# Attention and mixture-of-experts layer: the causal mask is added by VectorE in its maximum, and logits and the shared down product take fewer matmuls

## What is computed

```
q = x @ wq                                  # 8 heads of 128, 2 groups of keys and values
k = (x @ wk_down) @ wk_up;  v likewise      # through 32 latent features
scores = q @ k.T * scale                    # 1024 x 1024 for each head
scores = where(causal, scores, min)         # the mask
y = softmax(scores) @ v;  y @ wo

logits = x @ gate_weight.T                  # 32 experts
tw, topidx = top 6 of sigmoid(logits) + bias in the 2 best of 4 groups
routed = sum over experts of cw * (silu(x @ w_gate) * (x @ w_up)) @ w_down
shared = (silu(x @ shared_w_gate) * (x @ shared_w_up)) @ shared_w_down
anchor = the same with 16 smaller experts, the one that topidx names
```

## Time and profile before

| | us |
|---|---|
| median of three runs | 396.92 |
| the profiled execution | 394.98 |
| its span | 393.2 |
| TensorE busy | 374.4 |
| GpSimd busy | 284.0 |
| VectorE busy | 277.7 |
| ScalarE busy | 237.8 |

### The profile page before, as it was taken

How to read it: one execution, slowest core, us unless ns; L and a number is a source line. 1 busy time by engine, 2 the same in 40 slices (tenths; PEclk the granted TensorE clock), 3 DMA queues, 4 the chain that set the end, 5 groups by cost and what they waited for, 6 DMA issues and landing times.

```text
span 393.2 us, 6898 instructions
## 1 busy us (share of the span) xinstructions
PE 374.4 (95%) x2088; PEld 257.5 (65%) x2088; DVE 277.7 (71%) x707; ACT 237.8 (60%) x475; POOL 284.0 (72%) x336
## 2 busy tenths in 40 slices
PE   7989899999999998999999999999999999999992
PEld 7665455555555554455468887788878888788861
DVE  5979599986876983547348866759766677567674
ACT  4558566774745475844865556856565555665652
POOL 6126768299888799796597884899838997486651
PEclk9989899999999999999999999999999999999998
DMA  7299915805005005000000000000000000000000
GB/s 227 42 213 164 155 43 147 99 2 75 10 0 83 2 1 84 1 3 3 1 3 0 3 0 0 2 28 1 2 0 2 27 2 0 2 8 20 0 1 28
DMA packets 12691, 14.56 MB, mean 37 GB/s; under 512 B 1520, under 2 KB 9136, under 8 KB 12656
## 3 DMA queue, kind: packets, MB, share of 16 engines
q1 hardware_dynamic: 12096, 13.36, 18.1%
q10 hardware_dynamic: 560, 0.77, 0.6%
HBM read 6.26 MB, written 1.05 MB: 19 GB/s over the span
## 4 chain that ended last, share of the span: by engine, by line
PE 71%; POOL 11%; DVE 5%; issue 5%; DMA 3%; ACT 2%; POOLq 0%; ACTq 0%; DVEq 0%
PE ps L1342 11%; PE ps L1343 10%; PE ps L1344 10%; POOL probs L887 8%; PE ps L1442 7%; PE ps L1542 5%; PE ps L1460 5%; PE ps L1543 5%; PE ps L1544 5%; PE ps L1473 4%; PE ps L1483 3%; PE ps L1493 1%; DMA raw<-in_attn_wq 1%; PE ps L1445 1%; DMA qst<-shift_rows 1%
## 5 line engine op out<-in xcount | busy, mean ns | idle before, releaser
L960 POOL TENSOR_TENSOR silu<-silu,cwb 128x512 f32<-128x512 f32 x80 | 102.6, 1295 | 34.4 <-ACT silu L1113 30.3
L1239 DVE TENSOR_REDUCE nmax_h<-ps 128x1 f32<-128x512 f32 (+3 forms) x152 | 91.5, 654 | 30.5 <-PE ps L1445 15.8
L1083 ACT ACTIVATE probs<-ps 128x512 f32<-128x512 f32 (+1 forms) x152 | 78.4, 583 | 45.8 <-PE ps L1460 27.3
L887 POOL TENSOR_TENSOR probs<-probs 128x1024 f32<-128x1024 f32 (+3 forms) x56 | 92.4, 1671 | 16.1 <-PE ps L1473 12.1
L1113 ACT ACTIVATE silu<-ps 128x512 f32<-128x512 f32 x80 | 47.7, 598 | 47.4 <-PE ps L1344 41.4
L1306 DVE TENSOR_TENSOR ps<-silu,ps 128x512 f32<-128x512 f32 (+1 forms) x84 | 57.7, 693 | 24.3 <-POOL silu L960 23.5
L1313 DVE TENSOR_TENSOR h_lo<-ps,h_hi 128x512 fp32r<-128x512 f32 (+1 forms) x84 | 56.8, 685 | 25.5 <-ACT h_hi L1125 25.1
L1342 PE MATMUL ps<-xT_hi,w_hi 128*128 128x512 f32 x164 | 65.4, 399 | 0.0
L1442 PE MATMUL ps<-kst,qst 96*128 96x512 f32 (+3 forms) x192 | 63.9, 399 | 1.1 <-DVE nmax_h L1239 0.4
L1343 PE MATMUL ps<-xT_lo,w_hi 128*128 128x512 f32 x164 | 64.3, 392 | 0.0
L1460 PE MATMUL ps<-qst,kst 98*128 98x512 f32 (+1 forms) x152 | 60.4, 443 | 3.9 <-DMA qst<-shift_rows 3.2
(11 more groups left out here) (190 smaller groups left out, 495.9 us busy)
## 6 DMA issues: line engine op xcount, KB each, us to landing
qst<-q_hi SPq DMA_DIRECT2D x14, 256.0 KB, 5.4
qst<-q_lo SPq DMA_DIRECT2D x7, 256.0 KB, 6.9
x_sb<-in_attn_x SPq DMA_DIRECT2D x4, 256.0 KB, 6.3
raw<-in_ffn_w_gate SPq DMA_DIRECT2D x5, 192.0 KB, 4.8
raw<-in_ffn_w_up SPq DMA_DIRECT2D x5, 192.0 KB, 7.2
raw<-in_ffn_w_down SPq DMA_DIRECT2D x5, 192.0 KB, 3.5
kst<-k_hi SPq DMA_DIRECT2D x6, 128.0 KB, 7.1
result<-x_sb SPq DMA_DIRECT2D x3, 256.0 KB, 2.3
```

Of the source, the lines that this page charges most:

```text
L887: nc.gpsimd.tensor_tensor(into, into, probs[:, BUF[n, kt], j:end, cols], ALU.add).then_inc(added, 1)
L960: nc.gpsimd.tensor_tensor(silu[:, k % HRING, :], silu[:, k % HRING, :], cwb[:, m % 2, t // ET, :], ALU.mult).then_inc(scaled_ready, 1)
L1083: nc.scalar.activation(probs[:, BUF[n, kt], j:j + w, at:at + cols], bank(full)[:, 0:w * cols].rearrange("p (w c) -> p w c", w=w), ACT.Exp) ...
L1239: nc.vector.tensor_reduce(nmax_h[:, n % 2, i, j:j + w, h], bank(full)[:, 0:w * keys].rearrange("p (w k) -> p w k", w=w), AX.X, ALU.max, ne ...
```

## The change

It has five parts.

1. In blocks 1 to 7, for rows of 384 and 512 keys in the diagonal chunk, the mask matmul (L1445) is left out. VectorE's maximum becomes one `tensor_tensor_reduce` that reads scores and a row of mask (zeros, with the triangle in the last 128 columns), writes the masked scores back to PSUM and gives the negative maximum.
2. Logits: high and low half of the gate weight lie side by side, so hi by both is one matmul of 64 columns, and lo by hi one of 32: eight for a chunk where there were twelve. The two halves are added on VectorE by a new step `post_sum`, which the tanh now comes after.
3. The shared expert's `down` has two matmuls where it had three: its low half goes to partitions 64 to 127 of the same tile as the high half, under a second copy of the weight's high half (one more ACT copy of 64 partitions, once).
4. The maxima go by two DMAs of one row each where there was one of two rows.
5. Costs, three of the DMA times, the rank of `am2` and its copy, and the seed of the planner are other numbers.

```diff
+def masked_by_max(ev):
+    _, n, i, _, h, wide = ev
+    return h == BLOCKS[n][1] and wide == 1 and n > 0
...
-SEED, WOBBLE = 49, 0.04
+SEED, WOBBLE = 35, 0.04
...
-DMA_TIME = {"q_hi_dma": 390, "q_dma": 195, "q_far_dma": 195, "k_hi_dma": 170, "k_dma": 85, "s_dma": 15, "load": 90, "store": 80, "tail_store": 40}
+DMA_TIME = {"q_hi_dma": 390, "q_dma": 195, "q_far_dma": 195, "k_hi_dma": 170, "k_dma": 85, "s_dma": 65, "load": 60, "store": 80, "tail_store": 40}
...
-    step("PE", ("am2",), 60, 1.78, ("late_in",), bank=1, until=("m_copy",))
-    step("ACT", ("m_copy",), 45, 1.78, ("am2",))
+    step("PE", ("am2",), 60, 1.0, ("late_in",), bank=1, until=("m_copy",))
+    step("ACT", ("m_copy",), 45, 1.0, ("am2",))
...
-            step("DVE", peak, 15 + wide * cols * 104 // 1000, rank, ev, n >= 2 and ("nm_split", n - 2))
+            step("DVE", peak, 15 + wide * cols * 104 // 1000 + 18 * masked_by_max(ev), rank, ev, n >= 2 and ("nm_split", n - 2), ("consts",))
...
-        step("ACT", ("s_dma", n), 70, n + 0.9, ("shift_copy", n))
+        step("ACT", ("s_dma", n), 130, n + 0.9, ("shift_copy", n))
...
-        step("PE", ("post_logits", m), 130, rank, ("post_T_lo", m), ("gw_split",), bank=1, until=("post_tanh", m))
-        step("ACT", ("post_tanh", m), 28, rank, ("post_logits", m), prior and ("route", m - 1, 0))
+        step("PE", ("post_logits", m), 87, rank, ("post_T_lo", m), ("gw_split",), bank=1, until=("post_sum", m))
+        step("DVE", ("post_sum", m), 40, rank, ("post_logits", m), prior and ("route", m - 1, 0))
+        step("ACT", ("post_tanh", m), 28, rank, ("post_sum", m))
...
-        mask1 = sb("mask1", [P, P], BF16)
+        mask_row = sb("mask_row", [P, CH], BF16)
+        mask1 = mask_row[:, CH - P:]
...
+                    if a == 2 and t + 3 == MT:
+                        last = nc.scalar.activation(wd_hi[SI:P, SHARED, :], w_raw[0:SI, SHARED, :], ACT.Copy)
...
-                    act.dma_start(qst[QROWS:KROWS, n % QRING, :, :].bitcast(F32), shift_rows[:, n % 2, :].bitcast(F32)).then_inc(shift_in[n % QRING], 16)
+                    for a in range(SHIFTS):
+                        row = qst[QROWS + a:QROWS + a + 1, n % QRING, :, :].bitcast(F32).rearrange("a j (i q) -> a (j i) q", q=P)
+                        act.dma_start(row, shift_rows[REP * TPC * a:REP * TPC * (a + 1), n % 2, :].bitcast(F32)).then_inc(shift_in[n % QRING], 16)
...
+                    if masked_by_max(full):
+                        dve.wait_ge(masks, 3)
+                        scores = bank(full)[:, 0:keys]
+                        nc.vector.tensor_tensor_reduce(scores, scores, mask_row[:, CH - keys:CH], -1.0, BIG, ALU.add, ALU.min,
+                                                       nmax_h[:, n % 2, i, j:j + 1, h]).then_inc(max_ready, 1)
+                        continue
...
+                elif kind == "post_sum":
+                    m = ev[1]
+                    dve.wait_ge(misc_full, MISC["post_logits", m])
+                    if m >= 1:
+                        dve.wait_ge(route_done, ROUTE_STEPS * (m - 1) + 1)
+                    both = bank(("post_logits", m))[:, 0:2 * TPC * E].rearrange("p (t a e) -> p t e a", a=2, e=E)
+                    nc.vector.tensor_reduce(logits[:], both, AX.X, ALU.add).then_inc(logits_ready, 1)
...
-                    nc.vector.tensor_tensor(h_lo[0:rows, k % HRING, :], bank(("u", k))[0:rows], h_hi[0:rows, k % HRING, :].bitcast(F32), ALU.subtract).then_inc(h_lo_ready, 1)
+                    low = h_lo[0:rows, k % HRING, :] if k in ROUTED else h_hi[SI:P, k % HRING, :]
+                    nc.vector.tensor_tensor(low, bank(("u", k))[0:rows], h_hi[0:rows, k % HRING, :].bitcast(F32), ALU.subtract).then_inc(h_lo_ready, 1)
...
-                    if h == c:
-                        last = nc.tensor.matmul(s[:, :, P * i:P * i + P], ident_bf[:], mask1[:].unsqueeze(1).to_broadcast([P, w, P]), start=False, stop=True)
+                    if h == c and not masked_by_max(ev):
+                        last = nc.tensor.matmul(s[:, :, P * i:P * i + P], ident_bf[:], mask1.unsqueeze(1).to_broadcast([P, w, P]), start=False, stop=True)
...
-                        last = three(bank(ev)[:, E * t:E * t + E], (xT_hi[:, cols], xT_lo[:, cols]), (gwT_hi[:], gwT_lo[:]))
+                        own = bank(ev)[:, 2 * E * t:2 * E * t + 2 * E]
+                        nc.tensor.matmul(own, xT_hi[:, cols], gwT[:].rearrange("p a e -> p (a e)"), start=True, stop=False)
+                        last = nc.tensor.matmul(own[:, 0:E], xT_lo[:, cols], gwT[:, 0], start=False, stop=True)
...
-                    nc.tensor.matmul(sums(m)[:], wd_hi[0:rows, t, :], hi, start=(t == 0), stop=False)
-                    nc.tensor.matmul(sums(m)[:], wd_hi[0:rows, t, :], lo, start=False, stop=False)
-                    nc.tensor.matmul(sums(m)[:], wd_lo[0:rows, t, :], hi, start=False, stop=(t == MT - 1)).then_inc(down_done, 1)
+                    nc.tensor.matmul(sums(m)[:], wd_hi[:, t, :], hi, start=(t == 0), stop=False)
+                    if k in ROUTED:
+                        nc.tensor.matmul(sums(m)[:], wd_hi[:, t, :], lo, start=False, stop=False)
+                        nc.tensor.matmul(sums(m)[:], wd_lo[:, t, :], hi, start=False, stop=False).then_inc(down_done, 1)
+                    else:
+                        nc.tensor.matmul(sums(m)[:], wd_lo[0:SI, t, :], hi[0:SI], start=False, stop=True).then_inc(down_done, 1)
```

More of the change, by code:

```diff
@@ L350, in plan @@
             qs = [("q_dma", n)] if n else [("q0_lo", jj) for jj in range(j, j + wide)]
-            step("PE", ev, score_cost(wide, cols) + (15 + 4 * wide if h == c else 0), rank, *qs, *ks, ("consts",), bank=1, until=peak)
-            step("DVE", peak, 15 + wide * cols * 104 // 1000, rank, ev, n >= 2 and ("nm_split", n - 2))
+            step("PE", ev, score_cost(wide, cols) + (15 + 4 * wide if h == c and not masked_by_max(ev) else 0), rank, *qs, *ks, ("consts",), bank=1, until=peak)
+            step("DVE", peak, 15 + wide * cols * 104 // 1000 + 18 * masked_by_max(ev), rank, ev, n >= 2 and ("nm_split", n - 2), ("consts",))
         step("DVE", ("nm_split", n), 55, n + 1, *[("max", *ev[1:]) for ev in steps], n >= 1 and ("shift", n - 1), bank=1, until=("shift_copy", n))
@@ L435, in plan @@
         step("DVE", ("lo", k), 69, rank - 2, ("hi", k), *(lies_over(2 * HRING + k) if k < HRING else []))
-        step("PE", ("down", k), 68, rank - 3, ("lo", k), k >= 1 and ("down", k - 1), bank=0 if t else 1, until=("fin_copy", m) if m < NCH - 1 else ("tail_copy", 1))
+        step("PE", ("down", k), 68 if t != SHARED else 45, rank - 3, ("lo", k), k >= 1 and ("down", k - 1), bank=0 if t else 1, until=("fin_copy", m) if m < NCH - 1 else ("tail_copy", 1))
     for m in range(NCH - 1):
@@ L562, in build @@
         normed_p = sb("normed_p", [P, TPC, D])
+        logits = sb("logits", [P, TPC, E])
         enx = sb("enx", [P, TPC, E])
@@ L682, in build @@
         ylat_ready = sem("ylat_ready")
+        logits_ready = sem("logits_ready")
         route_done = sem("route_done")
@@ L1085, in _ @@
                     m = ev[1]
-                    act.wait_ge(misc_full, MISC["post_logits", m])
-                    if m >= 1:
-                        act.wait_ge(route_done, ROUTE_STEPS * (m - 1) + 1)
-                    nc.scalar.activation(enx[:].rearrange("p t e -> p (t e)"), bank(("post_logits", m))[:, 0:TPC * E], ACT.Tanh, scale=0.5).then_inc(copied, 1)
+                    act.wait_ge(logits_ready, m + 1)
+                    nc.scalar.activation(enx[:].rearrange("p t e -> p (t e)"), logits[:].rearrange("p t e -> p (t e)"), ACT.Tanh, scale=0.5).then_inc(copied, 1)
                 elif kind == "route":
@@ L1191, in _ @@
                     dve.wait_ge(small_in, 16)
-                    halves(gwT_hi[:], gwT_lo[:], smallT[:, 2 * E:3 * E]).then_inc(gw_ready, 1)
+                    halves(gwT[:, 0], gwT[:, 1], smallT[:, 2 * E:3 * E]).then_inc(gw_ready, 1)
                 elif kind == "up_scale":
@@ L1536, in _ @@
                     m, t = divmod(k, MT)
-                    rows = P if k in ROUTED else SI
                     pe.wait_ge(h_lo_ready, H_LO["lo", k])
```

17 lines of the change are left out of this document (8 added, 9 removed).

## The result

The changed kernel takes **405.01 us** (median of 4, 404.21 to 405.98) against 397.77 for the kernel before beside it (median of 4, 394.61 to 399.95): ratio 1.0189, 95% interval 1.0113 to 1.0266. It is 1.9% slower, where 0.9% faster was forecast, and it lies outside the range of 388.3 to 399.3.

A forecast was written before the change was run, and what follows sets the result against it. TensorE's matmuls were taken as the bound in the mixture of experts and from 95 to 140, only partly elsewhere. -3.5 - 1.4 - 0.9 + 1.2 + 1.2 = -3.4 us from 396.92 gave 393.5; range 388.3 to 399.3.

The forecast's parts named there:

- the term "+1.2 us" for two DMAs: Attention: the second DMA's issue delays the maxima 0.64 us in two exposed blocks, +1.2 us; bounds 0 and 5.1.
- Rival C: Attention: VectorE bounds 50 to 95 and longer waits for the maxima lower TensorE's clock; 400 to 402.8 us, chance 0.13.
- The masks, TensorE (-3.5): Attention: 56 mask matmuls of 0.12 us left out, 6.7 us, counted by stretch as 3.5 us saved; bounds 1.6 and 6.7.
- VectorE (+1.2): Attention: each new maximum costs VectorE 0.11 us more; 16 from 50 to 95 counted as +1.2 us, bounds 0 and 3.2.
- "6 to 9" us of VectorE: Sign expected in the changed kernel's trace: VectorE's busy time up by 6 to 9 us.
- my shares by stretch: Matmul savings count fully in the mixture and 95 to 140, about a third from 50 to 95, under half from 140.
- Logits (-1.4): Four fewer logit matmuls of 0.11 us in each of four chunks: 0.5 us in attention, 0.9 in the mixture of experts.
- shared down (-0.9): Shared expert's down: four matmuls of 0.23 us go, 0.9 us saved, all on the path.
- Order (0, -2 to +2): Whole kernel: single steps shift a few places, nothing crosses a stage; counted 0, bounds -2 and +2 us.
- Rival D: The new seed packs the same steps 1 to 3 us worse, attention ends unchanged; 395 to 398 us, chance 0.15.
- Rival B: TensorE bounds all of attention, VectorE's and ACT's additions hide; 9.4 us saved, 387.5 to 391 us, chance 0.18.
- Rival E: VectorE's new instruction takes two passes, 0.6 us more for each of 56; 410 us or more, chance 0.04.

The follow-up runs named there:

- e4_one_dma_old_constants: Changed kernel with one DMA for the maxima and the seed, DMA times and ranks of the kernel before: 397.86 us, ratio 0.9999 to the kernel before.
- e12: e9 with the masks of the narrow score tiles added on TensorE again, same order: 396.55 us, ratio 0.9968 to the kernel before.
- e9: Changed kernel with one DMA for the maxima, and block n's queries held until block n-2's maxima have landed: 391.92 us, ratio 0.9854.
- e1_one_dma: Changed kernel in its own order with one DMA of two rows for the maxima again: 392.61 us, ratio 0.9844 to the kernel before.
- e10_fill_resized: Changed kernel with 13, 17, 15, 5 and 6 identity products on TensorE ahead of the five waits for the maxima: 397.91 us, ratio 1.0016.
- e6_hold_queries: Changed kernel, both DMAs kept, with block n's queries held until block n-2's maxima have landed: 393.31 us, ratio 0.9893 to the kernel before.
- e3_masks_only: Kernel before with part 1 alone, masks of narrow tiles added by VectorE, one DMA, its old constants: 404.70 us, ratio 1.0239.

## Why the prediction was wrong, point by point

**The step that failed is part 4, the term "+1.2 us" for two DMAs, with its bounds of 0 and 5.1.** It priced the delay of the *issue*, 0.64 us for each exposed block. What counts is the landing of the last DMA: it comes 0.25 us later when the queue of the sync engine is quiet and 1.2 to 3 us later when 768 KB of queries go out at the same time (the time that TensorE sees is later still), and it turned two waits into five. The term measured 12.4 us (405.01 less 392.61; 13.7 by the two ratios), some 7 of it the clock. Leave part 4 out, and the forecast was 396.92 - 4.6 = 392.3; the run without it gave 392.61. That this agrees to 0.3 us is partly luck: the kernel before was 2.4 us slower beside it, the ratio's interval holds no change at all, the masks' term in the sum was off by 2.3 us, and with the old constants (`e4_one_dma_old_constants`) the same three parts gave nothing.

The rows for it were there: the earlier trace rows showed two of eight landings exposed with one DMA, up to 1.7 us, and the earlier trace rows a DMA share of 1.07 around block 1. The issues in the same trace tell what these two blocks had that the other six had not: the first of the queries' transfers is issued 0.35 us ahead of the maxima, where in blocks 3 and 4 it is 0.51 and 0.45 us behind, and in the others 2 us behind or absent. A second DMA, 0.6 us behind the first, had to fall among the queries in four blocks. The prediction took both waits as the DMA's own duration and gave SP's queue no part in them.

**Rival C** (slower, 400 to 402.8, chance 0.13) named the right second half: the DMA exposed in more than four blocks, and a fall of the clock behind the wait. It was five. Its first half is wrong: VectorE from 50 to 95 had room, 36.4 of 45. Its price, 0.64 for a block and one fall of 1.5 us, was too small for the same reason as the forecast's.

**The masks, TensorE (-3.5) and VectorE (+1.2).** The sum of -2.3 was measured as -4.6 (`e12` against `e9`, where the maxima are not late). VectorE's side is the mis-sized one. Two instructions, as the Trainium skill had it (VectorE: DVE Perf Modes, Two Vector instructions with no wait between them); the trace gives the second 144 ns, inside my 83 to 186, and the first 720 and 578, not 693 and 560. But they don't add: the next instruction starts beside the read. VectorE's busy time rose by 3.6 us, of which 1.7 are the logits' sum; (3.6 - 1.7) / 56 = 0.03 us for each maximum (0.05 between `e9` and `e12`, which differ in the masks alone: 281.6 and 278.9 us), where 0.11 was counted and "6 to 9" us of VectorE in all was what I said would show it. With that, -3.5 + 0.3 would have been forecast; the last 1.4 us are TensorE's share of the 6.7, which my shares by stretch put too low, if the 4.6 is right to a microsecond.

**Logits (-1.4) and shared down (-0.9).** The part of both that lies behind attention was forecast at 0.9 + 0.9 = 1.8. From the first product of the mixture's stream behind attention's last to the final product:

```profile
202.28 0.50 PE L1342 MATMUL ps<-xT_hi,w_hi 128*128 128x512 f32 x1
...
386.05 0.71 PE L1558 MATMUL ps<-ident,oT 128*128 128x128 f32 x4 [0.47 <-ACT oT L1138]
```

```profile
215.44 0.50 PE L1367 MATMUL ps<-xT_hi,w_hi 128*128 128x512 f32 x1
...
397.25 1.11 PE L1587 MATMUL ps<-ident,oT 128*128 128x128 f32 x4 [0.47 <-ACT oT L1149]
```

183.8 us before (first fence), 181.8 in the changed kernel: 2.0 us, near the forecast's 1.8. But the two stretches do not hold the same work. The changed order has left 161 groups of three products of `g` and `u` for it, the order before 160, and such a group takes 0.7 us: for the same work it is 2.7 us. With the old constants (`e4_one_dma_old_constants`) there are 159 groups in 181.6 us, 1.5 us less than before for the same work. So the order moves this figure by a microsecond, and 1.8 is right only to that. The first of these rows also shows attention ending 13.2 us later.

**Order (0, -2 to +2).** `e4_one_dma_old_constants` and `e1_one_dma` differ in it alone: 0.9999 and 0.9844, the new order ahead by 1.5%, 5 us by the medians, with an interval on the second wide enough for none. It has 2.9 us of waits for the maxima against 6.1, so that most of it, if it is there, may be the same collision once more and not the packing; no run parts the two. The term of 0, with bounds of 2 us, may so be too small as well. Rival D, an order that packs worse, did not happen. Rival B (TensorE bounds attention, 9.4 us for parts 1 to 3) asks for a ratio of 0.976 where part 4 and the collision are gone, the forecast for 0.988: `e9_one_dma_hold` has 0.9854 [0.9784, 0.9924], which leaves B's full price outside and cannot part the forecast from a B with some of it lost (up to 391, 0.985). Its support was slightly misread as well: TensorE's share from 10 to 50 is 36.72 of 40, 91.8% and not over 92. Rival E did not happen: the new instruction makes one pass.

**What stays open.** Waits and clock don't add up as two prices. To `e1_one_dma` (392.6) some 11 us of fill in the place of waits, at full clock, add 5 (`e10_fill_resized`); a lower mean clock with hardly a wait adds 1 (`e6_hold_queries`, 0.969); both together add 12 (the changed kernel). In `e9_one_dma_hold`, the profiled execution was slow in two stretches with no more than 0.5 us of waits for the maxima, and was still 394.7:

```profile
25.00:35.00 10.00, 9.39 (x31) 0.50 0.86 190
50.00:65.00 15.00, 11.79 (x45) 0.69 0.70 127
```

Slow time right behind a long wait, where TensorE is the one that is late, may cost more than slow time elsewhere: that would fit and was not tried. Not tested either was what starts those slow stretches, and with them the spread of the kernel before from 394 to 407. That the late landing in block 4 explains the 2.4% of `e3_masks_only` is argued from its trace: that kernel was not run with the queries held back. And that the small transfer is late where the bulk is issued first is seen in all of blocks 1 to 5, but the runs do not show what delays its packets.

## What to carry to other kernels

Price a small DMA on the critical path by its landing under the traffic of that moment, not by its issue: list for each block what the other queues issue within a microsecond of it, and take the exposed cases as the price of each, not the median. Splitting one such DMA in two cost 0.25 us a block where nothing was near and 3 to 5% of the kernel beside bulk transfers. An order that moved the bulk issue of one block from 0.45 us behind the small DMA to 0.73 ahead of it made a wait of 3.6 us with a single DMA. One wait that holds the bulk transfer until the small one has landed (it was needed two blocks later) took the loss away with both DMAs in place. Where TensorE's clock falls behind its waits, as here, count for the clock about as much again as for the waits.
